# 16-head attention in a four-layer kernel: where the products for the maxima stand in TensorE's order

## The reference, cut to what matters

```python
energy = jnp.einsum('nqhd,nkhd->nhqk', q, k)
attn = jax.nn.softmax(energy / jnp.sqrt(jnp.float32(EMBED_DIM)), axis=3)
out = jnp.einsum('nhql,nlhd->nqhd', attn, v).reshape(N, -1, H * Dh)
return out @ Wo.T + bo
```

## Time and profile before

| what | value |
|---|---|
| median of 3 runs | 3855.08 us (3851.18 to 3855.32) |
| the profiled execution's own time | 3853.51 us |
| its span, first to last instruction | 3851.8 us |
| TensorE busy (matmul) | 3547.0 us, 92% |
| VectorE busy | 2496.2 us, 65% |
| ScalarE busy | 1561.1 us, 41% |
| mean granted clock of TensorE | 0.940 of full |
| the 16-head attention stage | from about 253 to 1600 us |

### The profile page before, as it was taken

The page is one execution under the profiler, slowest core; times in us unless marked ns, Lnnn a source line. Parts: engine busy times, 40 slices in busy tenths (PEclk is TensorE's granted clock), DMA queues, the critical chain, the costliest instruction groups (busy, mean ns, idle before and its releaser), DMA issues. The chain is left out here.

```text
span 3851.8 us, 67359 instructions
## 1 busy us (share of the span) xinstructions
PE 3547.0 (92%) x21964; PEld 2075.7 (54%) x21964; DVE 2496.2 (65%) x5809; ACT 1561.1 (41%) x2718; POOL 207.3 (5%) x242
## 2 busy tenths in 40 slices
PE   8958999999999999896996899996999999999999
PEld 5631222222222222265884445454898898888888
DVE  4548887878778788232012344443888888888886
ACT  4525676767767677501221122221222222222221
POOL 0020000000000000011001000000000000000000
PEclk9978999999999999856997999996999999999999
DMA  6676454554544542041112113113000000000000
GB/s 222 232 199 84 68 73 62 71 75 60 73 71 60 74 70 32 25 150 47 38 35 88 57 56 96 51 56 143 10 11 11 11 11 11 12 10 11 12 10 9
DMA packets 144067, 240.15 MB, mean 62 GB/s; under 512 B 22793, under 2 KB 100082, under 8 KB 143346
## 3 DMA queue, kind: packets, MB, share of 16 engines
q1 hardware_dynamic: 134626, 220.54, 26.3%
q0 software_dynamic: 4608, 12.59, 1.0%
q10 hardware_dynamic: 4624, 4.46, 0.3%
HBM read 170.25 MB, written 66.86 MB: 62 GB/s over the span
## 5 line engine op out<-in xcount | busy, mean ns | idle before, releaser
L574 DVE TENSOR_REDUCE at_pmax<-at_psm 128x2 f32<-128x800 f32 (+1 forms) x1024 | 965.6, 988 | 258.1 <-PE at_psm L438 248.8
L528 ACT ACTIVATE at_pr<-at_pss 128x512 f32<-128x512 f32 (+1 forms) x1664 | 906.7, 598 | 331.9 <-PE at_pss L452 329.4
L452 PE MATMUL at_pss<-at_qs,at_ks 99*128 99x512 bf16 (+1 forms) x1664 | 584.2, 395 | 26.3 <-issue 18.9
L1611 PE MATMUL mt_psd<-mt_xl,mt_key_in 128*128 128x128 f32 x4096 | 493.2, 279 | 0.0
L1611 PEld LDWEIGHTS mt_psd<-mt_xl,mt_key_in 128*128 128x128 f32 x4096 | 471.8, 193 | 1.4
L460 PE MATMUL at_pso<-at_pr,at_vw 128*32 128x512 f32 (+1 forms) x3328 | 450.0, 612 | 0.0
L1637 PE MATMUL mt_psu<-mt_key_out,mt_g 128*128 128x256 f32 x2048 | 447.4, 379 | 1.3 <-DVE mt_g L1859 1.3
L452 PEld LDWEIGHTS at_pss<-at_qs,at_ks 99*128 99x128 bf16 (+1 forms) x1664 | 136.1, 98 | 559.9 <-ACT at_pr L528 406.7
L436 PE MATMUL at_psm<-at_ks,at_qs 64*128 64x400 bf16 (+1 forms) x1024 | 360.0, 352 | 75.3 <-DMA at_qs<-q_dram 35.6
L1637 PEld LDWEIGHTS mt_psu<-mt_key_out,mt_g 128*128 128x128 f32 x2048 | 386.7, 190 | 52.6 <-DVE mt_g L1859 1.4
L438 PE MATMUL at_psm<-at_kh,at_qh 64*128 64x400 bf16 (+1 forms) x1024 | 359.8, 352 | 0.0
(11 more groups left out here) (223 smaller groups left out, 3889.2 us busy)
## 6 DMA issues: line engine op xcount, KB each, us to landing
at_ks<-k_dram SPq DMA_DIRECT2D x192, 200.1 KB, 6.4
k_dram<-pj_kp SPq DMA_DIRECT2D x24, 800.5 KB, 5.4
v_dram<-pj_v SPq DMA_DIRECT2D x8, 1664.0 KB, 8.7
at_vd<-v_dram SPq DMA_DIRECT2D x32, 416.0 KB, 9.7
pj_ctx<-ctxT SPq DMA_DIRECT2D x8, 1601.0 KB, 11.3
at_kh<-k_dram SPq DMA_DIRECT2D x128, 100.1 KB, 5.4
aw_ctxT<-ctxT SPq DMA_DIRECT2D x8, 1601.0 KB, 7.3
at_qs<-q_dram SPq DMA_DIRECT2D x192, 64.0 KB, 6.6
```

The source lines that it names most:

```text
L452: nc.tensor.matmul(ps_s[0:r, (NST * g + n) % SBANKS, :], ks[:, g, j, kt * P:kt * P + r], qs[:, g, j, :], start=True, stop=True).then_inc(s ...
L528: nc.scalar.activation(pr[0:r, (NST * g + n) % PRING, :], ps_s[0:r, (NST * g + n) % SBANKS, :], ACT.Exp, scale=SCALE).then_inc(expd, 1)
L574: nc.vector.tensor_reduce(pmax[:, 2 * p:2 * p + 2, q, c:c + 1], ps_m[:, n % MBANKS, :, 0:MSPANS[c][1]], AX.X, ALU.max).then_inc(m_red, 1)
L1611: ins = nc.tensor.matmul(ps_d[:, j % 2, y * P:y * P + P], key_in[:, k, j * YB + y, :], xl[:, s, k, :], start=k == 0, stop=k == KC - 1)
```

## The change

The spread over tiles goes away. A function `maxima(slot)` is called twice in each step: between the second and the third score (even slots, one pair) and behind the value products (odd slots, two pairs). In steps 1 to 9 it issues the next unit's pairs as long as there are any, from step 11 on the early pairs of the unit after next, 8 instead of 10. The place of `turn_max` stays at step 10. So the order of a step, with s a score, p a pair, v the value products and T the transpose of the maxima, goes from

```diff
--- before.py
+++ after.py
@@ -337,10 +337,10 @@
     SCALE = 1.0 / float(D) ** 0.5
     UNITS = B * G
     NLOAD = 2 * len(Q_PART) + 2 * MAX_PARTS
-    INVERT_IN, INVERT_AT = 3, 15
-    EARLY, EARLY_AT = 10, 42
-    MAX_SPREAD = 38
-    TURN_AT = MAX_SPREAD // HG + 1
+    INVERT_IN, INVERT_AT = 3, (15, 19)
+    EARLY, EARLY_AT = 8, 20
+    TURN_AT = 10
+    LEAD = HG // 2
     with Stage(nc, "at") as st:
         ks, qs = st.sb("ks", [STACK, SLOTS, HG, KEYS], BF16), st.sb("qs", [STACK, SLOTS, HG, S], BF16)
         kh, qh = st.sb("kh", [P, SLOTS, HG // 2, KEYS], BF16), st.sb("qh", [P, SLOTS, HG // 2, S], BF16)
@@ -474,24 +474,31 @@
                     u = b * G + g
                     nxt, over = ((b, x) if x < G else (b + 1, x - G) if b is not last else None for x in (g + 1, g + 2))
                     done, early = EARLY, 0
+
+                    def maxima(slot):
+
+                        nonlocal done, early
+                        for _ in range(1 + slot % 2):
+                            if slot < 2 * TURN_AT - 2:
+                                if nxt is not None and done < len(max_jobs):
+                                    max_product(nxt[0], nxt[1], u + 1, done)
+                                    done += 1
+                            elif slot >= EARLY_AT:
+                                if over is not None and early < EARLY:
+                                    max_product(over[0], over[1], u + 2, early)
+                                    early += 1
+
                     for kt in range(1, KT + 1):
                         if kt == KT and nxt is not None:
                             pe.wait_ge(ones, nxt[1] + 1)
                             pe.wait_ge(m_in, u * 48 + 97)
                         for j in range(HG):
-                            tile = HG * (kt - 1) + j + 1
+                            if j == LEAD:
+                                maxima(2 * kt - 2)
                             if kt < KT:
                                 scores(u, g, kt * HG + j)
                             elif nxt is not None:
                                 scores(u + 1, nxt[1], j)
-                            todo = min(len(max_jobs), EARLY - (EARLY - len(max_jobs)) * tile // MAX_SPREAD)
-                            while nxt is not None and done < todo:
-                                max_product(nxt[0], nxt[1], u + 1, done)
-                                done += 1
-                            todo = max(0, EARLY * (tile - EARLY_AT) // (NST - EARLY_AT))
-                            while over is not None and early < todo:
-                                max_product(over[0], over[1], u + 2, early)
-                                early += 1
                         if nxt is not None and kt == TURN_AT:
                             turn_max(u + 1)
                         if kt == 1:
@@ -500,6 +507,7 @@
                             pe.wait_ge(acc_out, u + 1)
                         for j in range(HG):
                             values(u, g, (kt - 1) * HG + j)
+                        maxima(2 * kt - 1)
 
                 last = B - 1
                 for n in range(len(max_jobs)):
@@ -568,14 +576,16 @@
                 def maxima(u, me, behind=None):
 
                     for n, (p, q, c) in enumerate(max_jobs):
-                        if behind is not None and INVERT_AT <= n < INVERT_AT + 4 * INVERT_IN and (n - INVERT_AT) % 4 == 0:
-                            invert(behind, me, (n - INVERT_AT) // 4)
+                        if behind is not None and n in INVERT_AT:
+                            invert(behind, me, INVERT_AT.index(n))
                         dve.wait_ge(m_mm, u * len(max_jobs) + n + 1)
                         nc.vector.tensor_reduce(pmax[:, 2 * p:2 * p + 2, q, c:c + 1], ps_m[:, n % MBANKS, :, 0:MSPANS[c][1]],
                                                 AX.X, ALU.max).then_inc(m_red, 1)
                     dve.wait_ge(m_red, (u + 1) * len(max_jobs) + MBANKS)
 
                     nc.vector.tensor_reduce(nmax[:, :], pmax[:, :, :, :].rearrange("p j q c -> p (j q) c"), AX.X, ALU.max, negate=True).then_inc(m_all, 1)
+                    if behind is not None:
+                        invert(behind, me, INVERT_IN - 1)
                     dve.wait_ge(m_turned, u + 1)
 
                     dve.wait_ge(m_in, u * 48 + 1)
```

## The result

The changed kernel takes 3877.4 us in the median of its runs (3871.1 to 3881.8), against 3855.1 us before: a ratio of 1.0057, 95% interval 1.0044 to 1.0071, so 22 us slower. The profiled execution took 3881.8 us, the slowest of them; its span is 3880.1 us where the one of before is 3851.8.

A forecast was written before the change was run, and what follows sets the result against it. TensorE's in-order queue sets the pace, VectorE close behind. 24 units at +1.05 (25.2), turn units 3.9, last but one +2.6, prologue −1.8: +29.9 to +31 on 3853.5, forecast 3886 us, range 3858 to 3908.

The forecast's parts named there:

- Costs in TensorE's order: TensorE's start-to-start times: value products to pair 1.00 us, pair to pair 0.17; moved pairs alone make a step 2.91, against 3.03.
- (a): Rival: value products to pair costs only 0.91 us, so the unit is 39.4, time +5, 3860; chance 0.10.
- (c): Rival: a pair next to the value products costs as much as between scores (1.10): +62, some 3917; chance 0.09 with worse.
- Part 2, the bank wait: ps_m's two banks: a pair waits for the reduction two before; TensorE stands still 0.45 us, steps take 3.26 us.
- A to M': From the first of two pairs behind the value products to the next but one: at least 1.44 us, 0.99 without the wait.
- Rival (b): Bank wait does not bind, reductions ending sooner: below 1.33 us unit under 39.3; at 0.99 about 36.9, time −70; chance 0.11.
- Part 3: Steps 9 and 10, without pairs: the fourth score waits for the first's exponential, so 2.46 us instead of 2.0.
- Part 4: Transpose of the maxima and inversion pieces: the wait of just under 0.5 us per unit goes; line 562's transpose costs TensorE 0.27.
- The price named for a lost cover: Second inversion transpose (line 566), moved behind the final maximum beside step 9: nothing, or 0.7 ahead of the mpart copies if uncovered.
- The sum for a unit: Steps of one head group added up: 40.29 us against 39.32 measured before, between +0.97 and +1.1, taken as +1.05.
- The units with a turn: Six units in which the batch loop turns: low clock partly hides the bank wait, +0.65 each, 3.9 us.
- The prologue: Ahead of the stage's first scores: two pairs fewer to reduce, at 0.90 us each, saving 1.8 us.

The follow-up runs named there:

- half reductions: Each maxima reduction reads 200 of a head's 400 columns: changed kernel so altered 3776.7 us, kernel before so altered 3805.4 us.

## Why the prediction came out, and where it did not

The forecast was 3886 us, +31; measured is 3877, +22, inside the range, and on the side forecast. The mechanism came as described; two terms were too large.

- **Costs in TensorE's order.** Value products to pair: 1.00 taken, 0.998 in 330 of 336 places, so (a) and (c) fall. Pair to pair: 0.17 taken, 0.18 measured.
- **Part 2, the bank wait.** 1.44 from A to M' and steps of 3.25, as said. The waits sum to 107.3 us in 273 places where 120 and 270 were expected. The 0.39 of one is not a smaller delay than the 0.45 set: it counts from the modelled end of the score ahead. Without the wait the pair at 907.11 would have started at 906.67 (905.67 + 0.18 + 0.27 + 0.23 + 0.32), which is 0.44 earlier. Rival (b) needed less than 1.33 us from A to M'. The half reductions bring it about: 37 us a unit, close to the 36.9 that (b) was worked out with.
- **Part 3.** Steps 9 and 10 show the fourth score's wait of 0.32; 63 such waits are 20.0 us. In step 11, where I had listed one more, the pair after the second score fills it.
- **Part 4.** The wait ahead of the transpose is gone. Step 10 was set at 2.67 and takes 2.57: from a score to the transpose it is 0.23 and not the 0.32 of a change of shape. The transpose of line 562 costs 0.27 (step 4 takes 3.53). The price named for a lost cover, 0.7 ahead of the copies, was the right size by luck (0.6) and the wrong path.
- **The sum for a unit** was 40.29, measured 40.18. The term +1.05 was mis-sized, with 0.86 measured. 0.10 of that is step 10. The rest is that I added part of the shortfall of my own sum for the present order (39.2 for 39.32) to the difference, though the sum for the new order had no such shortfall. It makes 0.19 × 23 = 4.4 us.
- **The units with a turn** were the step that failed outright: +0.65 each was set, −0.3 came, 5.7 us in all. From the last value products ahead of the turn to the third behind it the kernel before takes 14.45 us in the mean of the six and the changed one 14.00, where the normal steps for it would be 8.51 and 9.23. So 1.17 us disappear, where one bank wait less, 0.4, was set. Most of it is the first of these steps, with the gap and the low clock behind it: 7.61 before and 6.41 changed, 1.20 apart where normal first steps (3.05 and 2.74) are 0.31 apart. The new order has one pair in it instead of three, so less work is left where the clock is low. That is read from the timelines; no run separates the clock from the pairs.
- **The prologue**, −1.8: the reductions do not end last there, a DMA does; in the profile that the forecast was built on they did, by 0.8 us.

Unit and turn together overshoot by 10.1 us, and the prologue's missing 1.8 goes the other way: 8.3 in all, about the distance of the forecast from the median (8.6).

## What to carry to other kernels

A ring of two buffers is not a rate but a distance: with hand-ordered issue the test is not whether the consumer keeps up on average (VectorE was idle 0.46 us a step here) but whether each producer stands at least one consumer's latency, 1.44 us here, behind the one two before it. Where a wait can't be avoided, put as little as possible behind it in an in-order queue, and use the places where the queue waits for someone else anyway: a pair there cost nothing (step 11 with it takes 2.46 us, as steps without pairs do). When a piece of work is moved, look also at what it releases on other engines, and whom that meets.

## What the runs showed of the hardware

- A VectorE copy of 16x128 from SBUF to SBUF, fp32 to bf16, took 1.11 us while GpSimd ran a 1.27 us multiply of two SBUF tensors, and 0.21 us otherwise. Reductions from PSUM beside the same multiply took 0.99 us, as without it.
- Adjacent pairs on the two halves of TensorE's rows start 0.18 us apart; a change of shape in between costs 0.09 to 0.10 us, but none was seen from a score to the fp32 transpose with 16 columns (0.23 us, as from score to score).
- Where the loop turns, TensorE idles some 3 us for nothing that the profile names (17.6 us in 6 times), with the granted clock at 0.58 of full, near its lower level of 1.2 GHz, in the stretch around it. In the kernels tried here the six units with a turn are 4.2 to 5.9 us longer in the mean than the others.
